# Sums of odd groups in two banks, and an earlier close of each node tile, in a graph network layer

## The chip, the cores and the metric

The kernel runs on one core of a Trainium2 chip. The time is the device time of one execution in microseconds. The core's engines work side by side and meet at semaphores: TensorE (PE in the profile, with its weight loads as PEld), VectorE (DVE), ScalarE (ACT), GpSimd (POOL) and SyncE (SP, which here issues every DMA).

## The reference, cut to what matters

12,500 nodes with 128 features, 200,000 edges with 48 features. The edges are sorted by their target node `dst`. All is float32.

```python
def ref(x, edge_attr, dst, W1, b1, W2, b2, W3, b3):
    h = maximum(layernorm(x), 0)
    agg_edge = segment_sum(edge_attr, dst, num_segments=12500)
    collected = concatenate([h, agg_edge], axis=1)          # 128 + 48
    a = silu(collected @ W1 + b1)                            # 256
    a = silu(a @ W2 + b2)                                    # 256
    return x + h + (a @ W3 + b3)
```

## The kernel before, in words

**Tiles and groups.** Nodes are handled in 28 tiles of 448 (NT = 28, the last has 404). Edges are handled in 391 groups of 512, 14 groups to a batch, one batch to a node tile (29 batches, since the batches are shifted by four groups; the last one has three groups). For a group VectorE makes a one-hot matrix 42 nodes wide (`onehot`, L708, one instruction per half batch), and TensorE multiplies the edges by it: `sum_tile` (L1000). Even groups are added straight into a bank of `agg_ps` at the tile's own columns (L1020). Odd groups go to columns of their own in the PSUM bank `stage` (L1024), each of the seven pairs 42 columns. ScalarE copies all seven at once to `staged` in SBUF (`stage_sums`, L498 to L505), and GpSimd adds them one by one to `agg_carry`, a sum over all nodes (`add_odd`, L436 to L450). The first three of the seven (EARLY = 3) can reach back into the tile before, so that tile may only be closed when they are added; the other four wait until it is closed.

**Closing a tile.** `carry_over` (L845) on VectorE adds the bank and `agg_carry` to `agg` (L853) and passes the overhang on (L857). Then ScalarE rounds `agg` and VectorE makes the rest (`agg_lo`, L863), as `relu` (ScalarE, L542) and `relu_lo` (VectorE, L870) do for the normalised nodes. Both pairs feed layer 1.

**Steps.** Each engine has a function `step(i, turn)`, and works through its steps 1 to 30 in the order in which the code is written (steps 4 to 19 are a hardware loop of four steps a turn, the others are written out). No planner and no costs are involved; the engines wait for each other by semaphores alone. In step i TensorE does layer 2 of tile i-2, layer 1 of tile i-1, the sums of batch i+1, layer 3 of tile i-2 and the transposes of tile i. Layer 3 adds onto a bank into which ScalarE has put b3 (`seed_b3`, L550 to L556) and needs both halves of `h2` (`activate2`, L558). Layer 2 needs `h1` of the step before (`activate1`, L568). The transposes need `xn` (`normalize`, L525), which needs `rstd` (GpSimd, L425) and `nmr` (VectorE, L701). In the last steps some parts have run out: step 27 has a batch of three groups, steps 28 and 29 have no sums at all, and step 29 has no layer 1.

SyncE loads edges three steps ahead and stores results after `finish` (L890).

## Time and profile before

| what | value |
|---|---|
| median of 3 runs | 308.7 us (308.48 to 309.76) |
| the profiled execution's own time | 308.38 us |
| its span in the profile | 306.5 us (1.88 us lie around it) |
| TensorE busy / its weight loads | 287.6 us / 256.4 us |
| VectorE, ScalarE, GpSimd busy | 245.6, 224.8, 121.6 us |
| granted TensorE clock | full, but for 0.50 in two stretches before 46 us |

How to read it: a share of busy time says little by itself here, since a busy TensorE may be streaming or held. The timeline of the weight loads shows when TensorE truly begins each part of a step, and a bracket behind a row says how long the engine was idle before it and which instruction of which engine ended that. Durations that a row gives reach to the end of the instruction, and the next one on the same engine may start about 0.1 us before that end.

### The profile page before, as it was taken

What the parts mean: (1) busy time and instruction counts of PE and PEld (TensorE: products, weight loads), DVE (VectorE), ACT (ScalarE), POOL (GpSimd) and SP (SyncE); (2) the same over time, 40 slices, a digit from 0 to 9 for tenths busy, and PEclk for the clock granted to TensorE, in tenths of its full rate; (3) what the DMA queues carried; (4) which work ended last, traced back from release to release, by engine and by line L of the source; (5) the groups of instructions that cost most, each with busy time, mean ns of one, the idle gap of its engine ahead of it and who ended that gap; (6) DMA issues with size and microseconds to landing.
All of it is one profiled execution on the core that took longest, in us unless ns stands there. A gap on an engine that the chain in (4) does not pass through costs nothing.

```text
span 306.5 us, 12286 instructions
## 1 busy us (share of the span) xinstructions
PE 287.6 (94%) x4378; PEld 256.4 (84%) x4379; DVE 245.6 (80%) x620; ACT 224.8 (73%) x435; POOL 121.6 (40%) x240
## 2 busy tenths in 40 slices
PE   6973969999999999999999999999999999999994
PEld 5763849998899889988899888988899888999993
DVE  7788877798887988888888978888888988875560
ACT  8773667778767877778677877779777887779762
POOL 3055534343544345332443435333553435434200
PEclk9996979999999999999999999999999999999999
DMA  5998347556866578555864577555885568731111
GB/s 162 311 289 227 85 129 208 148 155 188 245 180 164 147 233 240 162 140 177 240 194 142 162 220 240 147 151 182 239 228 157 155 192 238 211 95 35 32 31 57
DMA packets 79218, 53.15 MB, mean 173 GB/s; under 512 B 2928, under 2 KB 78794, under 8 KB 79184
## 3 DMA queue, kind: packets, MB, share of 16 engines
q1 hardware_dynamic: 79184, 52.70, 59.8%
q8 instruction: 21, 0.34, 0.5%
q14 instruction: 13, 0.11, 0.1%
HBM read 46.29 MB, written 6.40 MB: 172 GB/s over the span
## 4 chain that ended last, share of the span: by engine, by line
PE 46%; issue 21%; POOL 16%; DVE 8%; POOLq 5%; ACT 1%; DVEq 1%; ACTq 0%
POOL agg_carry L450 12%; PE z L1089 10%; PE agg_ps L1020 10%; POOL rstd L425 4%; PE z L1073 4%; PE z L1077 4%; PE z L1074 4%; POOLq L430 3%; PE z L1053 3%; PE z L1058 2%; PE z L1055 2%; PE z L1059 2%; PE z L1054 2%; PE stage L1024 2%; PE tp L1037 2%
## 5 line engine op out<-in xcount | busy, mean ns | idle before, releaser
L450 POOL TENSOR_TENSOR agg_carry<-staged,agg_carry 48x42 f32 x195 | 80.3, 412 | 79.5 <-POOL agg_carry L450 30.1
L1020 PEld LDWEIGHTS agg_ps<-onehot,raw 128*48 128x48 f32 x1568 | 73.2, 125 | 11.4 <-issue 11.3
L708 DVE TENSOR_TENSOR onehot<-window,rel 128x1176 f32<-128x1176 f32 (+1 forms) x57 | 77.2, 1355 | 5.8 <-DVE stats L683 4.1
L1020 PE MATMUL agg_ps<-onehot,raw 128*48 128x42 f32 x1568 | 77.2, 214 | 1.9 <-DVE onehot L708 1.6
L1024 PE MATMUL stage<-onehot,raw 128*48 128x42 f32 x1560 | 76.9, 214 | 0.0
L425 POOL TENSOR_TENSOR rstd<-vareps,minus_half 112x4 f32<-112x4 f32 (+1 forms) x28 | 38.6, 1377 | 89.2 <-DVE vareps L693 89.2
L1024 PEld LDWEIGHTS stage<-onehot,raw 128*48 128x48 f32 x1560 | 72.8, 125 | 0.1
L1089 PE MATMUL z<-w,h 128*112 128x128 f32 (+1 forms) x448 | 56.1, 278 | 0.8 <-ACT h L563 0.8
L1089 PEld LDWEIGHTS z<-w,h 128*112 128x112 f32 (+1 forms) x448 | 50.5, 176 | 2.4 <-ACT z L555 1.1
L534 ACT ACTIVATE xn<-x_t,nmr,rstd 112x128 f32<-112x128 f32 (+1 forms) x112 | 45.8, 479 | 2.2 <-DVE nmr L701 2.2
L542 ACT ACTIVATE hT_hi<-tp 128x448 fp32r<-128x448 f32 (+1 forms) x28 | 15.2, 544 | 42.7 <-PE tp L1037 42.6
L853 DVE TENSOR_TENSOR agg<-agg_ps,agg_carry 48x448 f32<-48x448 f32 (+1 forms) x28 | 17.2, 615 | 34.3 <-POOL agg_carry L450 33.5
L1073 PE MATMUL z<-h_hi,w_hi 128*128 128x448 f32 (+1 forms) x112 | 43.3, 387 | 0.0
L1074 PE MATMUL z<-h_hi,w_lo 128*128 128x448 f32 (+1 forms) x112 | 40.8, 364 | 0.0
L877 DVE TENSOR_TENSOR h_lo<-h,h_hi 128x448 fp32r<-128x448 f32 (+1 forms) x56 | 34.8, 621 | 6.7 <-ACT h_hi L577 5.7
L573 ACT ACTIVATE h<-z,b1c 128x448 f32<-128x448 f32 (+1 forms) x56 | 35.0, 625 | 4.7 <-PE z L1059 4.0
L563 ACT ACTIVATE h<-z,b2c 128x448 f32<-128x448 f32 (+1 forms) x56 | 34.8, 621 | 3.1 <-PE z L1077 2.6
L577 ACT ACTIVATE h_hi<-h 128x448 fp32r<-128x448 f32 (+1 forms) x56 | 32.3, 576 | 1.8
L1077 PE MATMUL z<-h_lo,w_hi 128*128 128x448 f32 (+1 forms) x112 | 31.7, 364 | 0.0
L1053 PE MATMUL z<-hT_hi,w1x_hi 128*128 128x448 f32 (+1 forms) x56 | 23.4, 417 | 8.2 <-DVE hT_lo L870 5.3
L548 ACT ACTIVATE agg_hilo<-agg 48x448 fp32r<-48x448 f32 (+1 forms) x28 | 16.1, 576 | 17.5 <-DVE agg L853 17.4
L683 DVE BATCH_NORM_STATS2 stats<-x_t 112x6 f32<-112x128 f32 (+1 forms) x112 | 24.2, 279 | 0.0
(119 smaller groups left out, 435.8 us busy)
## 6 DMA issues: line engine op xcount, KB each, us to landing
raw<-in_edge_attr_dram SPq DMA_DIRECT2D x55, 672.0 KB, 5.5
x_t<-in_x_dram SPq DMA_DIRECT2D x27, 224.0 KB, 6.2
out_dram<-out_t SPq DMA_DIRECT2D x27, 224.0 KB, 5.8
dst_rows<-in_dst_dram SPq DMA_DIRECT2D x1, 512.0 KB
raw<-in_edge_attr_dram SPq DMA_DIRECT2D x1, 288.0 KB, 3.5
dst_rows<-in_dst_dram SPq DMA_DIRECT2D x1, 256.0 KB, 2.8
out_t<-in_L_gnn_W_dram SPq DMA_DIRECT2D x1, 256.0 KB, 7.4
x_t<-in_x_dram SPq DMA_DIRECT2D x1, 192.0 KB
```

The source lines that it names most:

```text
L425: pool.tensor_tensor(rstd[0:np_, parity], vareps[0:np_, :], minus_half[0:np_, :], ALU.pow).then_inc(s_rstd, 1)
L450: pool.tensor_tensor(into, staged[:, parity, k // 2, :], into, ALU.add).then_inc(s_odd, 1)
L534: ln = act.activation(xn[0:np_, parity, q, :], x_t[0:np_, turn, q, :], ACT.Identity, bias=nmr[0:np_, parity, q:q + 1], scale=rstd[0:np_, p ...
L563: act.activation(h2[:, m, 0:n], z[:, m, 0:n], ACT.Silu, bias=b2c[:, m:m + 1]).then_inc(s_h2, 1)
L573: act.activation(h1[:, m, 0:n], z[:, m, 0:n], ACT.Silu, bias=b1c[:, m:m + 1]).then_inc(s_h1, 1)
L708: return dve.tensor_tensor(onehot[:, slot, at * PER:n * PER, :], window[:, :].unsqueeze(1).broadcast_to([P, cols_n, WINDOW]), cols.unsquee ...
L1020: mm = pe.matmul(banks[0:ED, bass.ds(offsets[(k - first) // 2], WINDOW)], edges, into, start=False, stop=True, skip_group_check=True, tile ...
L1024: mm = pe.matmul(stage[ROW2:ROW2 + ED, pair * WINDOW:(pair + 1) * WINDOW], edges, into, start=(k == first and j == 0), stop=True, skip_gro ...
L1073: pe.matmul(z[:, m, 0:n], w2_hi[:, k, cols], h1_hi[:, k, 0:n], start=(k == 0), stop=False)
L1074: pe.matmul(z[:, m, 0:n], w2_lo[:, k, cols], h1_hi[:, k, 0:n], start=False, stop=False)
L1077: mm = pe.matmul(z[:, m, 0:n], w2_hi[:, k, cols], h1_lo[:, k, 0:n], start=False, stop=(k == M - 1))
L1089: mm = pe.matmul(z3[0:np_, q, :], h2[:, k, q * np_:(q + 1) * np_], w3[:, k, :], start=False, stop=(k == M - 1), skip_group_check=True)
```

## The change

The order of the work within a step is altered on three engines, and the bank `stage` is split in two.

1. Odd groups 0 to 2 of a batch stay in `stage`; odd groups 3 to 6 go to a new bank, `stage_end`. TensorE's order is the same.
2. ScalarE's one copy becomes two. `stage_first` copies three groups and waits only for the first half of the batch. `stage_rest` copies the other four when the batch is done. Between the two stand `seed_b3`, which stood between the two halves of `activate2`, and `normalize`, which stood before the copy. `clear_bank` now stands between the halves of `activate2`. Wait values follow the doubled count.
3. GpSimd does the three early additions before `rstd` instead of behind it.
4. VectorE closes the tile before it makes the first one-hot of a step (it stood behind it), and does `finish` behind `relu_lo` and `agg_lo` instead of ahead of them.

The core of the diff:

```diff
@@ add_odd, gpsimd
                     if k < 2 * EARLY:
-                        pool.wait_ge(s_staged, b + 1)
+                        pool.wait_ge(s_staged, 2 * b + 1)
...
                     else:
-                        pool.wait_ge(s_staged, b + 1)
+                        pool.wait_ge(s_staged, 2 * b + 2)
@@ step, gpsimd
                     nodes = nodes_of(i + 1)
+                    add_odd(i + 1, 1 - parity, nodes, True)
                 if has(i, -1, NT):
                     rstd_of(i + 1, 1 - parity)
                 if has(i, -1, NB):
-                    add_odd(i + 1, 1 - parity, nodes, True)
                     add_odd(i + 1, 1 - parity, nodes, False)
@@ scalar
+            def stage_first(t, parity):
+                act.wait_ge(s_summed, 2 * t + 1)
                 if not isinstance(t, int) or t > 1:
                     act.wait_ge(s_odd, odds_added(t - 1, 0))
-                act.activation(staged[:, parity].rearrange("d k w -> d (k w)"),
-                               stage[ROW2:ROW2 + ED, 0:STAGED],
+                act.activation(staged[:, parity, 0:EARLY].rearrange("d k w -> d (k w)"),
+                               stage[ROW2:ROW2 + ED, 0:EARLY * WINDOW],
+                               ACT.Copy).then_inc(s_staged, 1)
+
+            def stage_rest(t, parity):
+                act.wait_ge(s_summed, 2 * t + 2)
+                act.activation(staged[:, parity, EARLY:PAIRS].rearrange("d k w -> d (k w)"),
+                               stage_end[ROW2:ROW2 + ED, 0:(PAIRS - EARLY) * WINDOW],
                                ACT.Copy).then_inc(s_staged, 1)
@@ step, scalar
                 if has(i, 2, NT):
-                    activate2(i - 2)
+                    activate2(i - 2, 0)
                 if has(i, 1, NT - 2):
                     act.wait_ge(s_carried, i)
                     clear_bank(1 - parity)
+                if has(i, 2, NT):
+                    activate2(i - 2, 1)
                 if has(i, 1, NT):
                     activate1(i - 1)
-                if has(i, 0, NT) and not (isinstance(i, int) and i == NT - 1):
+                now = has(i, 0, NT) and not (isinstance(i, int) and i == NT - 1)
+                if has(i, -1, NB):
+                    stage_first(i + 1, 1 - parity)
+                if has(i, 2, NT):
+                    seed_b3(i - 2)
+                if now:
                     normalize(i, turn)
                 if has(i, -1, NB):
-                    stage_sums(i + 1, 1 - parity)
+                    stage_rest(i + 1, 1 - parity)
@@ step, vector
+                if has(i, 1, NT):
+                    carry_over(i - 1, 1 - parity)
                 if has(i, -2, NB) and not first:
                     make_onehot(i + 2, parity, 0)
                 if has(i, 1, NT):
-                    carry_over(i - 1, 1 - parity)
+                    relu_lo(i - 1)
+                    agg_lo(i - 1)
                 if has(i, 3, NT):
                     finish(i - 3, 1 - parity)
-                if has(i, 1, NT):
-                    relu_lo(i - 1)
-                    agg_lo(i - 1)
@@ sum_tile, tensor
-                wait(pe, s_staged, b)
+                wait(pe, s_staged, 2 * b)
...
-                                mm = pe.matmul(stage[ROW2:ROW2 + ED, pair * WINDOW:(pair + 1) * WINDOW], edges, into,
-                                               start=(k == first and j == 0), stop=True, skip_group_check=True,
-                                               tile_position=(0, ROW2))
+                                bank, col = (stage, pair) if pair < EARLY else (stage_end, pair - EARLY)
+                                mm = pe.matmul(bank[ROW2:ROW2 + ED, col * WINDOW:(col + 1) * WINDOW], edges, into,
+                                               start=((k == first or pair == EARLY) and j == 0), stop=True,
+                                               skip_group_check=True, tile_position=(0, ROW2))
```

ScalarE's row in a full step, from the second half of layer 2's activation to the copy of the sums (before; `h<-z,b2c` is `activate2`, `h<-z,b1c` and `h_hi` are `activate1`, `xn` is `normalize`):

```order
L555 ACTIVATE z<-b3r 112x512
L563 ACTIVATE h<-z,b2c 128x448
L480 ACTIVATE agg_ps<-zeros 48x512
L573 ACTIVATE h<-z,b1c 128x448
L577 ACTIVATE h_hi<-h 128x448
L573 ACTIVATE h<-z,b1c 128x448
L577 ACTIVATE h_hi<-h 128x448
L534 ACTIVATE xn<-x_t,nmr,rstd 112x128 x4
L503 ACTIVATE staged<-stage 48x294
```

The same stretch of the changed kernel:

```order
L481 ACTIVATE agg_ps<-zeros 48x512
L574 ACTIVATE h<-z,b2c 128x448
L582 ACTIVATE h<-z,b1c 128x448
L586 ACTIVATE h_hi<-h 128x448
L582 ACTIVATE h<-z,b1c 128x448
L586 ACTIVATE h_hi<-h 128x448
L508 ACTIVATE staged<-stage 48x126
L567 ACTIVATE z<-b3r 112x512
L545 ACTIVATE xn<-x_t,nmr,rstd 112x128 x4
L514 ACTIVATE staged<-stage_end 48x168
```

The write of b3 moved from ahead of four activations to behind them and behind the first copy, and the four instructions of `xn` stand behind it.

ScalarE's last rows, steps 28 and 29, before (step 28 begins with `hT_hi`, step 29 is the last three rows):

```order
L542 ACTIVATE hT_hi<-tp 128x404
L548 ACTIVATE agg_hilo<-agg 48x404
L563 ACTIVATE h<-z,b2c 128x448
L555 ACTIVATE z<-b3r 112x512
L563 ACTIVATE h<-z,b2c 128x448
L573 ACTIVATE h<-z,b1c 128x404
L577 ACTIVATE h_hi<-h 128x404
L573 ACTIVATE h<-z,b1c 128x404
L577 ACTIVATE h_hi<-h 128x404
L563 ACTIVATE h<-z,b2c 128x404
L555 ACTIVATE z<-b3r 101x512
L563 ACTIVATE h<-z,b2c 128x404
```

The same two steps of the changed kernel:

```order
L554 ACTIVATE hT_hi<-tp 128x404
L560 ACTIVATE agg_hilo<-agg 48x404
L574 ACTIVATE h<-z,b2c 128x448 x2
L582 ACTIVATE h<-z,b1c 128x404
L586 ACTIVATE h_hi<-h 128x404
L582 ACTIVATE h<-z,b1c 128x404
L586 ACTIVATE h_hi<-h 128x404
L567 ACTIVATE z<-b3r 112x512
L574 ACTIVATE h<-z,b2c 128x404 x2
L567 ACTIVATE z<-b3r 101x512
```

The write of b3 that layer 3 of step 28 waits for stands behind all four activations of layer 1, and that of step 29 behind both of layer 2.

VectorE's row from the end of one full step into the next, before (`h_lo` ends a step):

```order
L877 TENSOR_TENSOR h_lo<-h,h_hi 128x448
L708 TENSOR_TENSOR onehot<-window,rel 128x1176
L853 TENSOR_TENSOR agg<-agg_ps,agg_carry 48x448
L857 TENSOR_TENSOR agg_carry<-agg_ps,agg_carry 48x64
L895 TENSOR_TENSOR out_t<-z,resid 112x512
L870 SCALAR_TENSOR_TENSOR hT_lo<-tp,hT_hi 128x448
L863 TENSOR_TENSOR agg_hilo<-agg,agg_hilo 48x448
```

The same place in the changed kernel:

```order
L893 TENSOR_TENSOR h_lo<-h,h_hi 128x448
L869 TENSOR_TENSOR agg<-agg_ps,agg_carry 48x448
L873 TENSOR_TENSOR agg_carry<-agg_ps,agg_carry 48x64
L724 TENSOR_TENSOR onehot<-window,rel 128x1176
L886 SCALAR_TENSOR_TENSOR hT_lo<-tp,hT_hi 128x448
L879 TENSOR_TENSOR agg_hilo<-agg,agg_hilo 48x448
L911 TENSOR_TENSOR out_t<-z,resid 112x512
```

The close moved ahead of the one-hot, and the last sum of the output (`out_t`) behind the two that feed layer 1.

## Rows read from the trace of the kernel before

**Rows 1.** The page's busy times, first line.

```profile
PE 287.6 (94%) x4378; PEld 256.4 (84%) x4379; DVE 245.6 (80%) x620; ACT 224.8 (73%) x435; POOL 121.6 (40%) x240
```

**Rows 2.** Waits of weight loads, 49.9 to 284.1 us (total us, times, longest).

```profile
PEld z L1053 <- DVE hT_lo L870: 6.7, 19, 0.8
PEld z L1058 <- DVE agg_hilo L863: 1.2, 6, 0.3
```

**Rows 3.** Timeline of the weight loads: start us, us, engine, line, what [idle before].

```profile
49.95 0.19 PEld L1073 LDWEIGHTS z<-h_hi,w_hi 128*128 128x128 f32 x1
...
86.14 0.12 PEld L1020 LDWEIGHTS agg_ps<-onehot,raw 128*48 128x48 f32 x1 [0.30 <-issue]
...
88.76 0.19 PEld L1073 LDWEIGHTS z<-h_hi,w_hi 128*128 128x128 f32 x1
...
91.11 0.19 PEld L1053 LDWEIGHTS z<-hT_hi,w1x_hi 128*128 128x128 f32 x1
...
93.45 0.12 PEld L1020 LDWEIGHTS agg_ps<-onehot,raw 128*48 128x48 f32 x1 [0.30 <-issue]
...
96.10 1.03 PEld L1089 LDWEIGHTS z<-w,h 128*112 128x112 f32 x9
...
140.61 0.19 PEld L1053 LDWEIGHTS z<-hT_hi,w1x_hi 128*128 128x128 f32 x1 [0.76 <-DVE hT_lo L870]
...
274.39 0.19 PEld L1073 LDWEIGHTS z<-h_hi,w_hi 128*128 128x128 f32 x1
...
284.09 0.19 PEld L1073 LDWEIGHTS z<-h_hi,w_hi 128*128 128x128 f32 x1
```

**Rows 4.** Timeline of ScalarE near 138 us and in the step from 274.39.

```profile
137.89 0.55 ACT L542 ACTIVATE hT_hi<-tp 128x448 fp32r<-128x448 f32 x1 [1.72 <-PE tp L1037]
...
276.45 0.59 ACT L555 ACTIVATE z<-b3r 112x512 f32<-112x512 f32 x1
...
280.45 0.86 ACT L534 ACTIVATE xn<-x_t,nmr,rstd 112x128 f32<-112x128 f32 x2
...
282.11 0.41 ACT L503 ACTIVATE staged<-stage 48x294 f32<-48x294 f32 x1
```

**Rows 5.** Timeline of VectorE, 135 to 141 us.

```profile
135.92 1.38 DVE L708 TENSOR_TENSOR onehot<-window,rel 128x1176 f32<-128x1176 f32 x1
...
138.68 0.62 DVE L853 TENSOR_TENSOR agg<-agg_ps,agg_carry 48x448 f32<-48x448 f32 x1 [1.38 <-POOL agg_carry L450]
...
139.95 0.60 DVE L870 SCALAR_TENSOR_TENSOR hT_lo<-tp,hT_hi 128x448 fp32r<-128x448 f32 x1
```

**Rows 6.** Timeline of GpSimd, step 1 and around 254 us.

```profile
35.65 2.61 POOL L425 TENSOR_TENSOR rstd<-vareps,minus_half 112x4 f32<-112x4 f32 x1 [3.18 <-DVE vareps L693]
...
254.08 0.55 POOL L450 TENSOR_TENSOR agg_carry<-staged,agg_carry 48x42 f32 x1
...
254.89 0.25 POOL L450 TENSOR_TENSOR agg_carry<-staged,agg_carry 48x42 f32 x1 [0.25 <-POOL agg_carry L450]
```

**Rows 7.** Timeline of the weight loads, beginning of layer 1 in step 2.

```profile
41.43 0.19 PEld L1053 LDWEIGHTS z<-hT_hi,w1x_hi 128*128 128x128 f32 x1 [3.10 <-DVE hT_lo L870]
```

**Rows 8.** Busy times by stretch (columns: stretch, length, engines, clock, DMA).

```profile
42.00:45.20 3.20, 3.20 (x13) 2.42 (x12) 3.07 (x8) 2.08 (x5) 0.68 (x2) 0.50 0.02 5
```

**Rows 9.** Timeline of the weight loads, layer 3 in steps 27, 28 and 29.

```profile
289.64 0.49 PEld L1089 LDWEIGHTS z<-w,h 128*112 128x112 f32 x4
...
296.03 1.12 PEld L1089 LDWEIGHTS z<-w,h 128*112 128x112 f32 x9
...
301.09 1.02 PEld L1089 LDWEIGHTS z<-w,h 128*101 128x101 f32 x9 [1.08 <-ACT z L555]
```

**Rows 10.** Timeline of ScalarE in steps 27, 28 and 29.

```profile
290.28 0.41 ACT L503 ACTIVATE staged<-stage 48x294 f32<-48x294 f32 x1
...
297.08 0.54 ACT L577 ACTIVATE h_hi<-h 128x404 fp32r<-128x404 f32 x1
...
300.38 0.60 ACT L563 ACTIVATE h<-z,b2c 128x404 f32<-128x404 f32 x1
```

More of the change, by code:

```diff
@@ L186, in gnn_kernel @@
         stage = ps("stage", [P, BANK])
+        stage_end = ps("stage_end", [P, BANK])
         z = ps("z", [P, M, BANK])
@@ L498, in stage_sums @@
             def stage_sums(t, parity):
-                act.wait_ge(s_summed, 2 * t + 2)
+                stage_first(t, parity)
+                stage_rest(t, parity)
+            def stage_first(t, parity):
+                act.wait_ge(s_summed, 2 * t + 1)
                 if not isinstance(t, int) or t > 1:
                     act.wait_ge(s_odd, odds_added(t - 1, 0))
-                act.activation(staged[:, parity].rearrange("d k w -> d (k w)"),
-                               stage[ROW2:ROW2 + ED, 0:STAGED],
+                act.activation(staged[:, parity, 0:EARLY].rearrange("d k w -> d (k w)"),
[5 more added lines that the diff above has]
+                               stage_end[ROW2:ROW2 + ED, 0:(PAIRS - EARLY) * WINDOW],
                                ACT.Copy).then_inc(s_staged, 1)
@@ L523, in _, with normalize @@
                 act.activation(w1e_hi[a:a + ED, :], w1e_in[a:a + ED, :], ACT.Copy).then_inc(s_w_hi, 1)
-            def normalize(i, turn):
+            def normalize(i, turn, quarters=range(PER)):
                 np_ = nodes_p(i)
@@ L532, in normalize @@
                 wait(act, s_plain, i - 1)
-                for q in range(PER):
+                for q in quarters:
                     ln = act.activation(xn[0:np_, parity, q, :], x_t[0:np_, turn, q, :], ACT.Identity,
                                         bias=nmr[0:np_, parity, q:q + 1], scale=rstd[0:np_, parity, q:q + 1])
-                ln.then_inc(s_xn, 1)
+                if q == PER - 1:
+                    ln.then_inc(s_xn, 1)
             def relu(t):
@@ L556, in seed_b3, with activate2 @@
                                ACT.Copy).then_inc(s_seeded, 1)
-            def activate2(t):
+            def activate2(t, m):
                 n = PER * nodes_p(t)
-                for m in range(M):
-                    act.wait_ge(s_z2, M * t + m + 1)
-                    wait(act, s_z3, t)
-                    act.activation(h2[:, m, 0:n], z[:, m, 0:n], ACT.Silu,
-                                   bias=b2c[:, m:m + 1]).then_inc(s_h2, 1)
-                    if m == 0:
-                        seed_b3(t)
+                act.wait_ge(s_z2, M * t + m + 1)
+                wait(act, s_z3, t)
+                act.activation(h2[:, m, 0:n], z[:, m, 0:n], ACT.Silu,
+                               bias=b2c[:, m:m + 1]).then_inc(s_h2, 1)
             def activate1(t):
@@ L958, in general_path @@
             def general_path():
-                pe.wait_ge(s_staged, 2)
+                pe.wait_ge(s_staged, 4)
                 for rounds in range(2):
```

## The prediction

> **What bounds the kernel now.** I read the busy times first: TensorE is busy for 94% of the span, its weight loads for 84% [rows 1]. So the question is where TensorE is held, and the list of what its weight loads waited for answers it. In the 24 full steps from 49.95 to 284.09 [rows 3] it was 6.7 us for `hT_lo` and 1.2 us for `agg_hilo` [rows 2]; beside these there is only the 0.3 of issue at the head of each batch of sums (the 0.30 at 93.45 [rows 3]), which the change does not touch.
>
> Then the timeline of the weight loads [rows 3]. A step in which nothing is late begins at 88.76: layer 2 takes 2.35 (to 91.11), layer 1 2.34 (to 93.45), the sums 2.65 (to 96.10). Layer 3 and the transposes took 2.13 more, which I get from the step at 274.39 as well: 284.09 less 274.39 is 9.70, and a short pause in its sums makes up the difference to 9.47. So a step that is bound by TensorE alone takes 9.47. The 24 steps took 234.14, or 9.76 each. The excess is 234.14 - 24 x 9.47 = 6.9 us. The worst single case is at 140.61, 0.76 behind `hT_lo` [rows 3].
>
> Why is `hT_lo` late? VectorE's rows show it: it waits 1.38 for GpSimd's third early addition, closes the tile at 138.68 and only then, behind `out_t`, begins `hT_lo` at 139.95, which ends at 140.55 [rows 5]; the weight load starts 0.06 later. The early additions in turn stand behind ScalarE's copy of all seven sums, which stands behind `xn`, and behind `rstd`.
>
> **The change part by part.** Times within a step are counted from the first load of layer 2, in a step without waits.
>
> *First copy and additions.* ScalarE ends `activate1` at about 6.06 (280.45 less 274.39) [rows 3, 4]. The sums begin at 4.69; the first half is complete after 15 or 16 of 28 places, that is 1.45 later, plus about 0.25 for the matmul's own time and the semaphore (my estimate, from the 0.11 between the end of the activation at 300.98 and layer 3 at 301.09 [rows 9, 10] and as much again): 6.4. The copy of 294 columns took 0.41 [rows 4]; for 126 I take 0.27, of which the next instruction sees 0.2. So the early sums are in SBUF at 6.7 instead of at 282.11 + 0.41, which is 8.1 in that step. The additions take 0.25 each with 0.25 between them, or 0.55 where they meet VectorE [rows 6], so 1.3 to 1.9 for three: done by 8.0 to 8.6, and no `rstd` (1.0 to 2.6 [rows 6]) stands ahead of them. The close then takes 0.62 and 0.2, the one-hot 1.38 to its end and 1.3 to the next start, `hT_lo` 0.6 [rows 5]. With `hT_hi` ready at about 0.85 of the next step (it starts some 0.3 after layer 2 and takes 0.55 [rows 4]), `hT_lo` is done at about (8.6 + 0.8 + 1.3 + 0.6) - 9.47 = 1.8 at the latest. TensorE needs it at 2.35. The slack is 0.5 us or more, `agg_lo` follows 0.65 behind and is needed 0.6 later. So the waits of rows 2 for these two go. What is late next on VectorE: nothing that TensorE needs, since `out_t` ends by about 3.0 and b3 is written at 6.6.
>
> I credit 6.9 less 0.6 for two pauses inside the sums that have nothing to do with VectorE (0.30 at 86.14 [rows 3] and one more like it): **-6.3**. Bounds: 0 if the close is no earlier in effect, -6.9 if all goes.
>
> In the trace the additions take 0.55 beside a one-hot on VectorE and 0.25 clear of it [rows 6]. The Trainium skill (SBUF — State Buffer, Who interferes with whom) says that a VectorE instruction with two inputs in SBUF contends with a GpSimd instruction that reads SBUF, and that the loser blocks for the whole instruction. The trace agrees. It speaks against the new place of the additions, since they now meet both subtractions of `h_lo`, and `rstd` meets the one-hot. By it the close comes up to 0.6 later than by unhindered additions, which is inside the 8.6 above.
>
> *b3 and `xn` behind the first copy.* ScalarE's first copy must now wait until 6.4, so b3 is written from 6.6 to 7.2 (0.59 long [rows 4]) and layer 3 can begin 0.11 later, at 7.3. It wants to begin at 7.34 (96.10 less 88.76). That is no slack at all. I take a wait of 0.05 in each of 24 steps, **+1.2**; bounds 0 and 0.4 each (9.6), the upper one if the half-batch semaphore and the copy cost twice what I take. `xn` begins at 7.15 instead of 6.06 and lasts 1.66 (280.45 to 282.11 [rows 4]): done at 8.8, the transposes want it at 9.07. Hidden by layer 3, with 0.2 to spare. The second copy ends at 9.1; its four additions have until the next close, and its bank until the next batch. A second instruction of 0.2 on ScalarE costs nothing: it waits 1.72 for the transposes at 137.89 [rows 4], and as much in most steps. `clear_bank` between the halves of `activate2` sits in the time in which ScalarE waits for layer 2's second half.
>
> *Two banks.* The same matmuls in the same order; one more flag per batch. Nothing, between -0.2 and +0.2.
>
> *Steps 1 and 2.* Before, GpSimd spends 35.65 to 38.26 in `rstd` and adds only then [rows 6]; the close is late, TensorE idles 3.10 and begins layer 1 at 41.43 [rows 7]. Now the first copy of step 1 can be made at about 34.9, when the first half of batch 2 is done, and the additions follow at once. Meanwhile VectorE makes the two subtractions of `h_lo`, which can block them (I take 0.6 each, like `hT_lo` [rows 5]), so I take the close at 36.8 instead of 39.6, then the one-hot (1.3) and `hT_lo`, done at 39.45 instead of 40.85 + 0.5. Layer 1 begins at 39.5, **-2.0**. Against it: `xn` of tile 1 now waits for the half batch, and the transposes and layer 2 move back by 0.9, to 39.3; this still fits ahead of 39.5. Bounds -2.4 and 0.
>
> Behind the idle 3.10 the granted clock was 0.50 (1.2 GHz) for 3.2 us in which the weight loads were busy for 2.42 [rows 7, 8]. With an idle stretch of under 1 us there I expect the clock to stay at 2.4 GHz, and half of that busy time back: **-1.2**, bounds 0 and -1.6.
>
> *The last steps.* Here the cover of the moved b3 is gone. In step 27 the batch has three groups, and layer 3 began at 289.64, ahead of the end of `activate1`, whose end lets the copy start at 290.28 [rows 9, 10]. Now layer 3 waits for `activate1`, the first copy (0.2), b3 (0.59) and 0.11: 291.15, **+1.5**. In step 28 there are no sums: layer 3 began at 296.03, while the last activation of layer 1 ends at 297.62 [rows 9, 10]. Now b3 starts about 0.1 ahead of that end and ends at 298.1, so layer 3 begins at 298.2, **+2.2**, and layer 2 of the last tile stands behind it on TensorE. In step 29 the second `activate2` starts at 300.38 either way, held by layer 2; b3 now starts 0.5 behind it and ends at 301.45, so layer 3 moves from 301.09 to 301.55 [rows 9, 10]: **+0.4**. Nothing else covers these: TensorE has no other work there. Together +4.1, bounds +3 and +6; the upper one if the clock falls in the idle 2.2 of step 28 (it fell behind 3.10, and here the stretch is shorter, so I take that it doesn't; at half speed for as long as in rows 8 it would be +1.6).
>
> Sum: -6.3 + 1.2 - 2.0 - 1.2 + 4.1 = -4.2. Against the profiled execution's 308.38 (span 306.5 and 1.88 around it) that is 304.2. The median of the runs shown stands 0.3 above that execution; I predict 304.3.
>
> **The rivals.**
>
> *A. The close is no earlier in effect.* If GpSimd's additions are blocked by each VectorE instruction in turn, the close comes at 9.4 or later, and the one-hot that now stands ahead of `hT_lo` takes up what is left. Then the 6.3 is not won, and neither is the 1.2 lost: 304.3 + 5.1 = 309.4. For it: 0.55 and 2.61 in rows 6. Against it: VectorE idles 1.38 ahead of the close [rows 5], so it has room, and the work ahead of the additions shrinks by a copy and `rstd`.
>
> *B. Slower: layer 3 becomes bound by b3 in every step.* The place is ScalarE's queue between `activate1` and layer 3. The price is 24 times what b3 is late. At 0.4 a step it is 9.6 instead of 1.2, so 304.3 + 8.4 = 312.7. It decides from 0.3 a step on, where 7.2 - 1.2 = 6.0 eats the gain of 4.2 and the 0.5% above. For it: there is no slack by my sum, and the estimate of the half-batch semaphore rests on few rows. Against it: 0.3 is more than the whole copy.
>
> *C. The clock is not kept.* It falls in step 2 all the same, and again in step 28: +1.2 + 1.6, so 307.1. For it: both clocks fell behind idle stretches. Against it: both stretches are shorter than those.
>
> *D. b3 is never late in full steps and the two pauses go:* 304.3 - 1.2 - 0.6 = 302.5. The loss in the last steps stays.
>
> **How the numbers follow.** The forecast (302.8 to 306.5) gets 0.55, A 0.12, B 0.10, C 0.11, D 0.12. A measurement of this kernel can't tell less than about 0.5% (1.5 us) from no change, so faster is below 307.2 and slower above 310.2. The forecast, D and most of C are faster (0.77); A and the rest of C lie within (0.14); B is slower (0.09). The range 301.8 to 309.0 leaves out B and the upper part of A, and little below D.
>
> **What would show each step.** The list of TensorE's waits should have no `hT_lo` and no `agg_hilo` in the full steps, and layer 2 to layer 1 should be 2.35 each time. The three early additions should stand ahead of `rstd`, with the first at about 6.8 of the step. Layer 3 should show small waits for b3 (L567), 0 to 0.1; 0.3 or more is B. The steps should be about 9.5 long. Layer 1 of step 2 should begin near 39.5, at the full clock. In the last three steps layer 3 should wait about 1.5, 2.2 and 1.5 us in all for b3. I am wrong at the root if VectorE is at the close later than about 8.8 of a step, or if layer 3 in steps 27 and 28 does not wait.

## The result, and the profile after

The changed kernel takes 312.04 us (median of 7 runs, 310.74 to 313.19), the kernel before 308.7 (308.48 to 310.54). The ratio is 1.0102 with a 95% interval of 1.0071 to 1.0134: slower by 1%, where 304.3 was forecast. The profiled execution took 311.99, with a span of 310.0 at a mean granted clock of 0.982.

The first line of the page's busy times after, to set beside [rows 1]:

```profile
PE 285.9 (92%) x4378; PEld 256.7 (83%) x4379; DVE 249.0 (80%) x620; ACT 228.8 (74%) x464; POOL 122.1 (39%) x240
```

TensorE does the same work in more time: it is held for longer. This is what its weight loads waited for from 46 to 300 us (total us, times, longest; the same view as [rows 2]):

```profile
PEld agg_ps L1036 <- issue: 9.0, 27, 0.7
PEld z L1090 <- issue: 8.2, 16, 1.0
PEld z L1106 <- ACT z L567: 3.6, 2, 2.1
PEld z L1106 <- issue: 1.2, 2, 0.9
PEld stage_end L1041 <- issue: 0.3, 1, 0.3
PEld z L1070 <- ACT h L574: 0.2, 1, 0.2
```

`hT_lo` and `agg_hilo` are gone, as forecast. In their place stands a wait that the kernel before did not have there: L1090, a line of layer 2, 16 times, with "issue" as its cause, which means that no engine and no transfer released it. It sits between the two halves of layer 2. I call it the hole. The timeline of the weight loads shows it in the step from 134.83; the rows at 46.73 and 283.68 are the beginning of the first full step and the end of the last (columns as in [rows 3]):

```profile
46.73 0.19 PEld L1090 LDWEIGHTS z<-h_hi,w_hi 128*128 128x128 f32 x1
...
83.55 0.12 PEld L1036 LDWEIGHTS agg_ps<-onehot,raw 128*48 128x48 f32 x1 [0.56 <-issue]
...
134.43 0.44 PEld L1054 LDWEIGHTS tp<-ident,xn 112*128 112x128 f32 x4
134.83 0.19 PEld L1090 LDWEIGHTS z<-h_hi,w_hi 128*128 128x128 f32 x1
...
135.55 0.39 PEld L1094 LDWEIGHTS z<-h_lo,w_hi 128*128 128x128 f32 x2
136.94 0.19 PEld L1090 LDWEIGHTS z<-h_hi,w_hi 128*128 128x128 f32 x1 [1.00 <-issue]
...
138.06 0.19 PEld L1070 LDWEIGHTS z<-hT_hi,w1x_hi 128*128 128x128 f32 x1
...
283.68 0.19 PEld L1090 LDWEIGHTS z<-h_hi,w_hi 128*128 128x128 f32 x1
```

Layer 2 takes 138.06 - 134.83 = 3.23 here instead of 2.35. The second half, which normally starts 1.13 after the first, starts 2.11 after it. Of the 8.2 us, 7.5 lie in 13 of the 16 steps of the hardware loop (steps 4 to 19), and 0.7 in three of the eight full steps that are written out. From 46.73 to 283.68 the 24 full steps take 236.95 where they took 234.14 [rows 3].

```profile
131.81 0.28 ACT L508 ACTIVATE staged<-stage 48x126 f32<-48x126 f32 x1 [0.29 <-PE agg_ps L1036]
131.98 0.58 ACT L567 ACTIVATE z<-b3r 112x512 f32<-112x512 f32 x1
132.50 1.64 ACT L545 ACTIVATE xn<-x_t,nmr,rstd 112x128 f32<-112x128 f32 x4
134.04 0.29 ACT L514 ACTIVATE staged<-stage_end 48x168 f32<-48x168 f32 x1
```

`xn` ends at 134.14, 0.69 before layer 2 begins, and so it is in most steps. In the kernel before it ended 1.77 or 1.78 ahead in most. Here is one of its steps, first ScalarE and then the weight loads:

```profile
144.25 1.63 ACT L534 ACTIVATE xn<-x_t,nmr,rstd 112x128 f32<-112x128 f32 x4
```

```profile
147.67 0.19 PEld L1073 LDWEIGHTS z<-h_hi,w_hi 128*128 128x128 f32 x1
```

`xn` ends at 145.88, 1.79 ahead. The difference of 1.1 is what the first copy and b3, now ahead of `xn`, take.

VectorE and GpSimd did nearly what was forecast. GpSimd's first early addition and VectorE's rows for that step, to set beside [rows 5] and [rows 6]:

```profile
132.33 0.70 POOL L451 TENSOR_TENSOR agg_carry<-staged,agg_carry 48x42 f32 x1 [4.37 <-ACT staged L508]
```

```profile
134.30 0.62 DVE L869 TENSOR_TENSOR agg<-agg_ps,agg_carry 48x448 f32<-48x448 f32 x1 [1.39 <-POOL agg_carry L451]
134.84 0.20 DVE L873 TENSOR_TENSOR agg_carry<-agg_ps,agg_carry 48x64 f32 x1
134.98 1.36 DVE L724 TENSOR_TENSOR onehot<-window,rel 128x1176 f32<-128x1176 f32 x1
136.26 0.61 DVE L886 SCALAR_TENSOR_TENSOR hT_lo<-tp,hT_hi 128x448 fp32r<-128x448 f32 x1
```

`hT_lo` ends at 136.87, 1.2 before layer 1 wants it at 138.06; without this step's hole it would still be 0.3 early. The first addition took 0.70 beside VectorE's `h_lo` (132.29 to 132.91), and the next two 0.27 each.

The weight loads at the beginning of layer 1 in step 2, and of layer 3 in the last three steps, to set beside [rows 7] and [rows 9]:

```profile
39.68 0.19 PEld L1070 LDWEIGHTS z<-hT_hi,w1x_hi 128*128 128x128 f32 x1 [0.22 <-DVE hT_lo L886]
...
290.66 0.49 PEld L1106 LDWEIGHTS z<-w,h 128*112 128x112 f32 x4 [1.49 <-ACT z L567]
...
299.19 1.80 PEld L1106 LDWEIGHTS z<-w,h 128*112 128x112 f32 x16 [2.13 <-ACT z L567]
...
304.60 1.56 PEld L1106 LDWEIGHTS z<-w,h 128*101 128x101 f32 x14 [1.51 <-ACT z L567]
```

The change of the span by parts, forecast against measured:

| part | forecast | measured |
|---|---|---|
| start to layer 2 of step 3 (49.95, now 46.73) | -3.2 | -3.2 |
| waits for `hT_lo`, `agg_hilo` | -6.3 | -5.7 |
| b3 late in full steps | +1.2 | 0 |
| hole between the halves of layer 2 | 0 | +6.5 |
| other pauses in full steps (1.2 before, 3.2 after) | (in the 6.3) | +2.0 |
| last three steps and the end | +4.1 | +3.9 |
| sum | -4.2 | +3.5 |

The 6.5 is what layer 2 takes over 2.35 in each step, added up; the list says 8.2, since each of its idle times includes some 0.1 that is there without a hole. The other pauses are like the 0.56 at 83.55. They sit in the middle of the sums or of layer 3 and are also named "issue". In both kernels they lie in the same four steps, 6, 22, 25 and 26, and in the changed kernel in step 21 too; only step 6 belongs to the hardware loop.

### The profile page after: what moved, and what is told of

Read it like the earlier page. It is cut to its first block, busy times and chain, and to the rows that moved or that the text cites. A ratio compares the mean times of both kernels' runs of the same rounds, so it can differ in the third digit from the quotient of the medians.

```text
span 310.0 us, 12371 instructions
## 1 busy us (share of the span) xinstructions
PE 285.9 (92%) x4378; PEld 256.7 (83%) x4379; DVE 249.0 (80%) x620; ACT 228.8 (74%) x464; POOL 122.1 (39%) x240
## 4 chain that ended last, share of the span: by engine, by line
PE 86%; DVE 4%; ACT 3%; issue 3%; POOL 1%; ACTq 0%; POOLq 0%; DVEq 0%
PE agg_ps L1036 19%; PE z L1106 18%; PE z L1090 9%; PE z L1091 7%; PE z L1094 7%; PE z L1070 4%; PE z L1075 4%; PE z L1076 4%; PE z L1071 4%; PE z L1072 4%; PE tp L1054 3%; PE stage_end L1041 2%; PE stage L1041 1%; ACT agg_carry L490 1%; ACT h L582 1%
## 5 line engine op out<-in xcount | busy, mean ns | idle before, releaser
L451 POOL TENSOR_TENSOR agg_carry<-staged,agg_carry 48x42 f32 x195 | 90.5, 464 | 166.4 <-ACT staged L508 120.4
L574 ACT ACTIVATE h<-z,b2c 128x448 f32<-128x448 f32 (+1 forms) x56 | 35.5, 634 | 19.4 <-PE z L1094 17.2
L1090 PE MATMUL z<-h_hi,w_hi 128*128 128x448 f32 (+1 forms) x112 | 44.8, 400 | 2.8 <-issue 2.4
L1041 PE MATMUL stage_end<-onehot,raw 128*48 128x42 f32 x896 | 45.7, 214 | 0.5 <-issue 0.5
L1041 PEld LDWEIGHTS stage_end<-onehot,raw 128*48 128x48 f32 x896 | 42.8, 125 | 0.3 <-issue 0.3
L1041 PE MATMUL stage<-onehot,raw 128*48 128x42 f32 x664 | 35.6, 215 | 0.0
L1041 PEld LDWEIGHTS stage<-onehot,raw 128*48 128x48 f32 x664 | 32.2, 125 | 0.0
L426 POOL TENSOR_TENSOR rstd<-vareps,minus_half 112x4 f32<-112x4 f32 (+1 forms) x28 | 29.4, 1049 | 1.2 <-DVE vareps L709 1.2
L1090 PEld LDWEIGHTS z<-h_hi,w_hi 128*128 128x128 f32 x112 | 21.1, 188 | 9.1 <-issue 8.2
```

Of the source, the lines that this page charges most:

```text
L451: pool.tensor_tensor(into, staged[:, parity, k // 2, :], into, ALU.add).then_inc(s_odd, 1)
L574: act.activation(h2[:, m, 0:n], z[:, m, 0:n], ACT.Silu, bias=b2c[:, m:m + 1]).then_inc(s_h2, 1)
L1041: mm = pe.matmul(bank[ROW2:ROW2 + ED, col * WINDOW:(col + 1) * WINDOW], edges, into, start=((k == first or pair == EARLY) and j == 0), sto ...
L1090: pe.matmul(z[:, m, 0:n], w2_hi[:, k, cols], h1_hi[:, k, 0:n], start=(k == 0), stop=False)
```

## The experiments

The theory that I put forward, called R: the register load stands in the queue behind the wait for `xn`. From `xn`'s end it needs about 2.3 us until the second half of layer 2 can start (134.14 to 136.94 is 2.80, most others 2.2 to 2.4), and the second half is wanted at +1.13. Before, 1.78 + 1.13 = 2.91 covered it; now 0.69 + 1.13 = 1.82 doesn't. The rivals say that the pause has nothing to do with where the load stands (S), or that only the number of matmuls around the load matters and not the wait for `xn` (T).

**The load behind all of layer 2.** This is the edit of the changed kernel, cut to the step; the call between the halves goes too:

```
-                    offsets = layer2(i - 2, i + 1 if has(i, -1, NB) else None)
-                elif has(i, -1, NB):
+                    layer2(i - 2)
+                if has(i, -1, NB):
                     offsets = offsets_of(i + 1)
```

> The changed kernel, but TensorE's sequencer loads the seven offsets of the next batch behind all of layer 2 instead of between its halves. Theory R (the load stands behind the wait for xn in TensorE's queue; xn now ends 0.7 us ahead of layer 2 instead of 1.8, and the second half of layer 2 can't begin until 2.3 us after xn): the idle of L1090 (8.2 us in 16 places) goes, the steps come to about 9.5, time 312.0 - 6 = 306. Rival S (the hole in layer 2 has nothing to do with where the load stands, but with xn's or b3's timing on ScalarE itself, or with the second bank): the idle stays at 8 us in all, time 312. The 5 us of waits for b3 in the last three steps stay under both.

Measured: 304.93 (303.66 to 308.06), ratio to before 0.9884 (0.985 to 0.9917). The four longest waits from 46 to 300 us:

```profile
PEld agg_ps L1036 <- issue: 8.4, 26, 0.8
PEld z L1102 <- ACT z L567: 5.1, 3, 2.1
PEld z L1102 <- issue: 1.4, 2, 0.9
PEld z L1070 <- DVE hT_lo L886: 0.9, 1, 0.9
```

No line of layer 2 is left, and none of layer 1 waits for issue. All of layer 2 now stands ahead of the load and covers it: layer 1 is due 0.69 + 2.35 = 3.04 behind `xn`, and not 1.82 as the second half was. So the hole was the load, and without it the changed kernel is 1.2% faster than before instead of 1% slower.

**The same move in the kernel before.** The same edit.

> The kernel before, with the same one move of the load behind layer 2. Theory R: there the load is hidden already (xn ends 1.8 us ahead of layer 2 and 0.5 of slack is left), so nothing is won: 308.7, within 0.3%; the waits for hT_lo stay at 6.7 us in the full steps. Rival: if the place of the load costs something by itself, this one gets faster too, by 2 us or more.

Measured: 308.5 (306.0 to 310.18), ratio 0.9979 (0.9944 to 1.0014), no change that can be told. Its wait for `hT_lo`:

```profile
PEld z L1053 <- DVE hT_lo L870: 7.7, 21, 0.8
```

The load's old place cost the kernel before nothing that can be told. It became wrong by the change.

**The load ahead of the transposes.** It is ahead of the wait for `xn`; the transposes move to the head of the next step, ahead of layer 2, so that their order against layer 2 is the same. The edit, cut:

```
+                if has(i, -1, NB):
+                    offsets = offsets_of(i + 1)
+                if has(i, 1, NT):
+                    transposes(i - 1, 1 - parity)
                 if has(i, 2, NT):
-                    offsets = layer2(i - 2, i + 1 if has(i, -1, NB) else None)
-                elif has(i, -1, NB):
-                    offsets = offsets_of(i + 1)
+                    layer2(i - 2)
...
-                if has(i, 0, NT):
-                    transposes(i, parity)
```

> The changed kernel, but TensorE's sequencer loads the offsets of the next batch ahead of the transposes and so ahead of the wait for xn; the order of the matmuls is the same. Theory R: the load no longer waits for xn, but still for b3 and the issue of layer 3 (b3 is ready 1.6 us earlier than xn), so it ends near the time at which the transposes want to begin: the hole of 8 us in layer 2 goes, and at most 0.2 us a step comes back as a hole ahead of the transposes. Time 305 to 309. Theory S (the hole is not the load's) is already out by the run with the load behind layer 2; a second rival, T (what helped there was only that twelve matmuls hide the load, and the wait for xn plays no part): then the hole comes up ahead of the transposes in full, 312 or more.

Measured: 304.75 (303.91 to 305.27), ratio 0.985 (0.9811 to 0.9889). Ahead of the wait for `xn` the load costs next to nothing either: there were 0.4 us of issue ahead of the transposes, once. T would have brought the hole back there in full. The load stands behind layer 3 and its wait for b3 in this run, so the wait for b3 doesn't make the hole either. What matters is the wait for `xn`.

**The load at the head of layer 2, in the kernel before.** Behind the transposes, ahead of both halves.

```
+                if has(i, -1, NB):
+                    offsets = offsets_of(i + 1)
                 if has(i, 2, NT):
-                    offsets = layer2(i - 2, i + 1 if has(i, -1, NB) else None)
-                elif has(i, -1, NB):
-                    offsets = offsets_of(i + 1)
+                    layer2(i - 2)
```

> The kernel before, with the load of the offsets at the head of layer 2, behind the transposes, so that none of layer 2's matmuls hide it. Theory R: TensorE can't begin layer 2 until 2.3 us after xn, which ended 1.8 ahead of it: a hole of 0.5 (1.0 in the first step of a loop turn) at the head of layer 2 in each of 26 steps, of which the waits for hT_lo (0.3 each) are absorbed: 308.6 + 13 - 7 = 315, with the waits for hT_lo nearly gone. If the wait for xn plays no part in when the load ends (it is done long before), no hole and 308.6.

Measured: 309.12 (308.66 to 310.29), ratio 1.0009 (0.9988 to 1.0029). A miss: 315 was expected. By a fixed 2.3, layer 2 should have started 0.5 late everywhere; from 46 to 300 us it waited for issue three times, 0.6 us in all. Here are `xn` and the start of layer 2 in one of the steps without a hole:

```profile
163.56 1.64 ACT L534 ACTIVATE xn<-x_t,nmr,rstd 112x128 f32<-112x128 f32 x4
```

```profile
166.97 0.19 PEld L1070 LDWEIGHTS z<-h_hi,w_hi 128*128 128x128 f32 x1
```

`xn` ends at 165.20, layer 2 starts 1.77 behind it and is not late. So the load is through within 1.8 of `xn` there, and the 2.3 is not its length. Between the halves it also has the first half of layer 2 ahead of it in the queue, which may be why it is through later there; no run separates this.

**The same place in the changed kernel.** The same edit, but here `xn` is 1.1 later.

> The changed kernel, with the load of the next offsets at the head of layer 2 (behind the transposes, ahead of both halves) instead of between its halves. In the kernel before, whose xn ends 1.78 us before layer 2, the same place cost nothing in most steps, so there the load was ready 1.8 us behind xn. R (the load is behind the wait for xn, and xn now ends only 0.69 before layer 2): layer 2 itself then starts 1.8 behind xn, 1.1 late, in each of 24 steps, where the hole in its middle took 0.33: +0.8 x 24 = +18, so about 330 us (320 to 335), and no hole between the halves. A rival, a pause that belongs to the place between the halves and has nothing to do with xn: the pause goes as it did when the load was moved behind layer 2, 305 us.

Measured: 333.5 (332.41 to 336.99), ratio 1.0816 (1.0735 to 1.0897). The rows of one step, first ScalarE and then the weight loads, and the start of layer 2 in a later step:

```profile
142.23 1.64 ACT L545 ACTIVATE xn<-x_t,nmr,rstd 112x128 f32<-112x128 f32 x4
```

```profile
144.16 0.44 PEld L1054 LDWEIGHTS tp<-ident,xn 112*128 112x128 f32 x4
146.44 0.19 PEld L1087 LDWEIGHTS z<-h_hi,w_hi 128*128 128x128 f32 x1 [1.83 <-issue]
...
243.69 0.19 PEld L1087 LDWEIGHTS z<-h_hi,w_hi 128*128 128x128 f32 x1 [0.44 <-issue]
```

The total is about what R gives (330 was expected), with 23.6 us of such holes in 23 places from 46 to 300 us, but the size is not constant. From `xn`'s end to layer 2 it is 2.57 here, between 1.45 and 2.97 in the steps of the hardware loop and between 1.25 and 1.62 in the written-out steps with a hole. No matmul of layer 2 uses the offsets, so it is the order of the queue that holds them. The same edit costs nothing that can be told in one kernel and 21 us in the other. Ahead of the load the end of `xn` lies 1.1 nearer to layer 2 (b3 is later too, but the run with the load ahead of the transposes rules its wait out). That is not all of it: in the loop the mean here is 2.0 behind `xn`, where 1.8 was enough in most steps of the kernel before.

**`xn` back ahead of the first copy and b3**, in the changed kernel, with the load left where it is:

```
+                if now:
+                    normalize(i, turn)
                 if has(i, -1, NB):
                     stage_first(i + 1, 1 - parity)
                 if has(i, 2, NT):
                     seed_b3(i - 2)
-                if now:
-                    normalize(i, turn)
```

> The changed kernel with xn back ahead of the first copy of odd sums and of b3 on ScalarE; the load stays between the halves of layer 2. R: xn ends 0.9 to 1.0 earlier, about 1.7 us before layer 2, so the load is through before the second half is due at +1.1, and the hole of 0.33 a step is gone: -8, 304 us, if the first copy, now 1.2 later, delays nothing; GpSimd's additions and the close shift by up to 0.8, the one-hot and hT_lo behind them too, which may bring back waits of 0.1 to 0.2 a step: 304 to 309. The rival (the pause has nothing to do with xn): the hole stays, 312 or above.

Measured: 333.22 (332.97 to 334.9), ratio 1.081 (1.077 to 1.0851). The hole is gone as R has it, and a loss that I had left out takes its place. Here are the weight loads of one step:

```profile
141.79 1.80 PEld L1106 LDWEIGHTS z<-w,h 128*112 128x112 f32 x16 [1.24 <-ACT z L567]
143.52 0.44 PEld L1054 LDWEIGHTS tp<-ident,xn 112*128 112x128 f32 x4
143.92 0.19 PEld L1090 LDWEIGHTS z<-h_hi,w_hi 128*128 128x128 f32 x1
...
145.05 0.19 PEld L1090 LDWEIGHTS z<-h_hi,w_hi 128*128 128x128 f32 x1
```

The second half starts 1.13 after the first again. But b3 now stands behind `xn` (1.64), and layer 3 waits for it in each of the 24 full steps, 29.3 us in all. Between `activate1` and layer 3 ScalarE has room for the copy and b3 and nothing more. So as long as b3 stays behind `activate1` and the load between the halves, either layer 3 or the load pays. The other pauses don't show in this run either: all full steps take 10.64 to 10.67.

**b3 back at its old place in every step** (between the halves of `activate2`), in the changed kernel:

```
                     activate2(i - 2, 0)
+                    seed_b3(i - 2)
+                    activate2(i - 2, 1)
                 if has(i, 1, NT - 2):
                     act.wait_ge(s_carried, i)
                     clear_bank(1 - parity)
-                if has(i, 2, NT):
-                    activate2(i - 2, 1)
...
-                if has(i, 2, NT):
-                    seed_b3(i - 2)
```

> The changed kernel, but b3 is written between the halves of activate2 in every step again, and clear_bank behind them, as before. Theory R: xn ends 0.5 us earlier in each step (1.2 ahead of layer 2), so the hole in layer 2 shrinks by 0.5 where it was 0.25 to 0.6 and to about 0.4 in the first step of a loop turn: 5 to 6 us less in the full steps; and the waits for b3 in the last three steps (5.1 us) go to about 1: time 312.0 - 5.5 - 4.1 = 302.5. Rival S (b3 has to do with the last steps alone): 308.

Measured: 322.23 (321.59 to 323.71), ratio 1.0451 (1.0389 to 1.0513). A miss of 20 us. ScalarE's timeline, then VectorE's, shows what I had not counted:

```profile
143.48 0.60 ACT L567 ACTIVATE z<-b3r 112x512 f32<-112x512 f32 x1 [0.97 <-DVE out_t L909]
144.02 0.62 ACT L574 ACTIVATE h<-z,b2c 128x448 f32<-128x448 f32 x1
```

```profile
142.69 0.69 DVE L909 TENSOR_TENSOR out_t<-z,resid 112x512 f32<-112x512 f32 x1
```

b3 overwrites the bank that `out_t` reads. The change moved `out_t` behind `hT_lo` and `agg_hilo`, so b3's old place is now too early by 0.97. It holds `activate2`'s second half, and layer 1 waits for that, 20.5 us in 24 waits. So with `out_t` where the change puts it, b3 did have to move; where to is the question.

**b3 at its old place in the last three steps only:**

```
+                tail = isinstance(i, int) and i >= NT - 1
                 if has(i, 2, NT):
                     activate2(i - 2, 0)
+                    if tail:
+                        seed_b3(i - 2)
...
-                if has(i, 2, NT):
+                if has(i, 2, NT) and not tail:
                     seed_b3(i - 2)
```

> The changed kernel, but b3 is written between the halves of activate2 in steps 27 to 29 alone. Both theories: only the last steps change, by the 1.5 + 2.1 + 0.4 us that layer 3 waited longer there: 312.0 - 4.0 = 308.0, and the hole in layer 2 of the full steps stays at 8 us. If the last steps are bound by something else in the end, less.

Measured: 309.26 (307.35 to 310.9), ratio 1.0027 (0.9994 to 1.0059). The medians show 2.8 of the 4.0 expected. From layer 2 of step 27 to the end of the span it is 22.4 in the kernel before, 26.3 in the changed one and 24.2 here, so 2.1 of the 3.9 are won back there (the span of the profiled execution is 3.8 shorter, but 1.7 of that lies ahead of step 27). The term of the last steps is real; the rest of it stays in another form, 1.27 and 0.75 us of waiting for `activate2`, which b3 holds up here too. The 1.08 for b3 in the last step was there before the change.

**The load behind layer 2, and b3 at its old place in the last three steps.** The two edits together:

> The changed kernel with the load behind layer 2, and b3 between the halves of activate2 in steps 27 to 29 alone. The two repairs are independent by my theory: 304.9 - 3.5 = 301.4. If they overlap (the last steps bound by something else), 303 to 305.

Measured: 302.68 (301.96 to 303.65), ratio 0.9797 (0.9755 to 0.9839). The gains of the two runs, 7.1 and 2.8, would give 302.1, so they add as far as this can tell; the 301.4 expected took 3.5 for the end.

**b3 behind both halves of `activate2`, ahead of `activate1`, and the load behind layer 2:**

```
                     activate2(i - 2, 1)
+                    seed_b3(i - 2)
                 if has(i, 1, NT):
                     activate1(i - 1)
...
-                if has(i, 2, NT):
-                    seed_b3(i - 2)
```

> The changed kernel with the load behind layer 2, and b3 written in every step behind both halves of activate2 and ahead of activate1. By the theory that b3 must only stand behind out_t (3.4 us into a step) and ahead of layer 3: activate1 starts 0.2 late, which the wait for the half batch hides, xn ends 0.5 earlier, the last steps are repaired: 301 to 302. If b3's wait for out_t holds up activate1 by more, as it held up the second half of activate2 when b3 stood ahead of that, layer 2 of the next step or the first copy gets late: 305 or more.

Measured: 301.65 (300.0 to 302.19), ratio 0.9765 (0.9728 to 0.9802), as expected, and the fastest median, though its interval overlaps with those of the run before it and of the next. There `out_t` is done when b3 is due, and the copy and `xn` follow `activate1` at once.

**That move of b3 alone**, the load left between the halves: one ScalarE instruction away from the changed kernel.

> The changed kernel with one ScalarE instruction moved: b3 behind both halves of activate2 and ahead of activate1, in every step; the load of the offsets stays between the halves of layer 2. xn then ends where it does in the run with both moves, 1.21 us before layer 2 instead of 0.69. R (the second half comes no earlier than some 2.3 behind xn, and is due at +1.13): the hole of 0.33 is gone, but for 0.1 or so and for the first step of a loop turn (0.4, 4 or 5 times): 2 to 4 us in all, where the changed kernel has 8.2; and b3 is ahead of layer 3 in the last steps, -3.8: 301.65 of the run with both moves + 1 to 3 = 303 to 305. The rival (the hole doesn't depend on when xn ends, only on the load standing between the halves): 8.2 of holes stay, and only the last steps gain: 308.

Measured: 302.32 (302.06 to 302.89), ratio 0.9803 (0.9753 to 0.9852). From 46 to 300 us these are its waits for b3 and in layer 2; behind them stand ScalarE and the weight loads of one step:

```profile
PEld z L1105 <- ACT z L567: 1.5, 1, 1.5
PEld z L1089 <- issue: 0.6, 2, 0.5
```

```profile
139.66 1.65 ACT L545 ACTIVATE xn<-x_t,nmr,rstd 112x128 f32<-112x128 f32 x4
```

```profile
142.41 0.19 PEld L1089 LDWEIGHTS z<-h_hi,w_hi 128*128 128x128 f32 x1
...
143.53 0.19 PEld L1089 LDWEIGHTS z<-h_hi,w_hi 128*128 128x128 f32 x1
```

`xn` ends at 141.31, 1.10 before layer 2, and the second half starts 1.12 after the first: no hole. L1089 is the line of layer 2 here, and 8.2 us of waits in 16 places have become 0.6 in 2, both in the first step of a loop turn. Nothing about the load or its place was touched. This is R's cause, and not its size: by a fixed 2.3 there should have been 2 to 4 us of holes and a time of 303 to 305. The edit moves b3 itself as well as `xn`, and layer 3's wait for b3 also stands ahead of the load; the run with the load ahead of the transposes rules that wait out.

## Why the prediction was wrong, point by point

**The failed step is this one:** "`xn` begins at 7.15 instead of 6.06 and lasts 1.66: done at 8.8, the transposes want it at 9.07. Hidden by layer 3, with 0.2 to spare." Its numbers hold. In the step from 125.23, `xn` ends at 8.91 and no transpose waits. What failed is that the step stops at the transposes and leaves out who else waits. I asked for the consumer of `xn`'s data and stopped there.
The trace before held a hint. Its step 2 has an `xn` that is late for another reason, and there the hole is. In these weight loads of the kernel before, `xn` ended 0.96 before 35.92, and the second half starts 1.31 after the first:

```profile
35.92 0.19 PEld L1073 LDWEIGHTS z<-h_hi,w_hi 128*128 128x128 f32 x1
...
37.23 0.19 PEld L1073 LDWEIGHTS z<-h_hi,w_hi 128*128 128x128 f32 x1 [0.19 <-issue]
```

It was a weak hint. In step 2 of the changed kernel `xn` ends only 0.39 ahead, and there is no hole.

Point by point:

- *First copy, additions, close.* Right: the waits of [rows 2] went. Their size was 5.7, not 6.3. The first addition began 7.10 into the step (132.33 less 125.23), where 6.8 was forecast. The close was later than my 8.6 (134.30 is 9.07 behind 125.23, in a step with a hole of 0.14), and past the 8.8 that I had called the root. It did no harm: `hT_lo` still had 0.3. So that sign of being wrong at the root was set too early, and rival A did not happen.
- *b3 in full steps.* Mechanism right (no slack), size wrong: I took 0.05 a step, and it was 0. In the step above b3 ends at 132.56 and layer 3 starts at 132.70, at the end of the sums. Rival B did not happen. It has the size of the result, 312.7, but not its cause.
- *Steps 1 and 2 and the clock.* Right: 39.68 for 39.5, and 3.2 for 3.2 in all. The exact match is luck, since in the runs of the kernel before and its edits step 3 begins between 48.72 and 49.95. From 36 to 40 us the granted clock is 1.00, and it is again from 283.68 to 305, behind the idle 2.13 of step 28: rival C did not happen.
- *Last steps.* Right: 1.49, 2.13 and 1.51 for 1.5, 2.2 and 1.5 (of the last one 1.08 was there before).
- *The sum.* The prediction puts its median 0.3 above the profiled execution, which gives 304.5 and not 304.3. Nothing hangs on this.
- *Other pauses.* I kept 0.6 and called the rest fixed; they were 1.2 before and 3.2 after. The run with one ScalarE instruction moved has 2.5, the run with both moves 1.3, and in the run in which layer 3 waits for b3 in every full step none shows. I made no run on them, and their cause is open.

Shown by runs: the hole is the register load (moved away, it goes), it is tied to the wait for `xn` (ahead of that wait the load is nearly free; with `xn` 0.4 to 0.6 earlier it is as well), and b3's place is what made `xn` too late. Not settled: why the load's end lies anywhere from 1.25 to 2.97 us behind `xn`, and why later in the hardware loop than outside it. The Trainium skill (Runtime: NRT & Kernel Launch, "Instruction fetch mechanics") puts a register load at some 200 ns per register and calls such loads round trips; it speaks of loads from HBM that the runtime inserts, while these offsets lie in SBUF. An estimate from it is 7 x 0.2 = 1.4 for a full step's offsets. The shortest cases here, 1.25 with the transposes included, are below that, so here the load takes less than 200 ns per register at times. No run varied the number of registers.

## What to carry to other kernels

And when an instruction moves, check also what it overwrites, and what has yet to read that: here b3 had to follow `out_t`, and the best place tried was the first one behind it, not the last one that layer 3 allows.

## What the runs showed of the hardware

- With TensorE's load of seven offsets into registers at the head of layer 2, layer 2 of the changed kernel starts 1.25 to 2.97 us behind the end of the activation that the transposes ahead of the load wait for (1.45 to 2.97 in the hardware loop, 1.25 to 1.62 in written-out steps with a hole). The transposes' 0.4 is included. From 46 to 300 us it held layer 2 up for 0.6 us in all in the kernel before, with 1.78 from `xn` to layer 2, and for 23.6 us in the changed one, with 0.69.
- Moving it ahead of that wait, or behind all of layer 2, hid it in all but one step.
- Where a GpSimd addition ran beside a VectorE subtraction (`h_lo`) it took 0.70 us, and the next two 0.27.
- Pauses without a releaser in the middle of the sums or of layer 3, four of five in written-out code, came to 1.2 us in one kernel and to 3.2 in the other, though their TensorE instructions are nearly the same. Where layer 3 waited some 1.24 for b3 in every full step, none showed.
